# One program per engine for attention and FFN, and the short matmuls of a step in one group

## The reference

```python
q, k, v = (_causal_dwconv(_silu(xn @ W), conv_w) for W, conv_w in ...)   # 4 taps
z, a, b = xn @ Wz, xn @ Wa, xn @ Wb
q, k = rope and l2-normalise per head
for s in range(4):                                   # lags
    attn = sum_d(q * lag(k, s)) * scale
    out += (attn * sigmoid(lag(a, s) * b))[..., None] * lag(v, s)
rms = rsqrt(mean(out * out over all 2048 channels) + eps)
s = (out * rms * norm_w * _silu(z)) @ Wout
hidden = relu((xn @ sign(up_weight).T) * up_scale)
g = _silu((hidden @ sign(down_weight).T) * down_scale * output_scale)
return x + s * g
```

## Time and profile before

| | us |
|---|---|
| median of 3 runs (lowest, highest) | 1383.82 (1382.62, 1384.70) |
| the profiled execution, device time | 1383.09 |
| its span, first to last instruction | 1381.0 |
| start, until the steps run evenly (from the start) | about 74 |
| even steps, 14.10 each | 74 to 934 |
| seam between attention and FFN | 934 to 974 |
| FFN, then output | 974 to 1202, 1202 to 1371 |

### The profile page before, as it was taken

One profiled execution on the slowest core, in us unless ns is written; L12 is line 12 of the kernel. 1 busy time (PEld: TensorE's weight loads), 2 busy tenths in 40 slices (PEclk: granted clock), 3 DMA queues, 4 the chain that ended last, 5 costly groups with the idle time before them and its releaser, 6 DMA issues. The chain is left out here.

```text
span 1381.0 us, 23144 instructions
## 1 busy us (share of the span) xinstructions
PE 1350.4 (98%) x6824; PEld 1140.7 (83%) x6824; DVE 988.1 (72%) x1529; ACT 737.9 (53%) x2209; POOL 333.3 (24%) x508
## 2 busy tenths in 40 slices
PE   6999999999999999999999999996999999999998
PEld 4788888888888888888888888885888888888886
DVE  7898998989999999999998999983122222234443
ACT  5656665656656666666566665652654434432221
POOL 6134242323333232323333332422000000000001
PEclk9999999999999999999999999997999999999999
DMA  8233434334344344343433434333421101156454
GB/s 287 62 87 86 101 78 115 93 85 97 95 93 100 85 104 102 80 100 83 108 93 85 100 85 108 78 75 74 152 96 50 46 23 47 36 186 188 129 174 157
DMA packets 123418, 138.79 MB, mean 101 GB/s; under 512 B 30704, under 2 KB 67568, under 8 KB 123120
## 3 DMA queue, kind: packets, MB, share of 16 engines
q1 hardware_dynamic: 114160, 121.48, 31.1%
q0 software_dynamic: 9216, 16.78, 7.1%
HBM read 62.58 MB, written 25.30 MB: 64 GB/s over the span
## 5 line engine op out<-in xcount | busy, mean ns | idle before, releaser
L1169 DVE TENSOR_TENSOR hid_lo<-relu,hid_hi 128x512 fp32r<-128x512 f32 x64 | 44.3, 693 | 172.8 <-ACT hid_hi L1115 172.8
L670 DVE SCALAR_TENSOR_TENSOR y_v<-u_v,cw_v,y_v 128x512 f32<-128x512 f32 x192 | 144.8, 754 | 29.0 <-ACT y_v L561 24.3
L670 DVE SCALAR_TENSOR_TENSOR y_k<-u_k,cw_k,y_k 128x512 f32<-128x512 f32 x192 | 145.2, 756 | 26.1 <-ACT y_k L561 19.2
L581 ACT ACTIVATE bank<-bank 128x128 f32<-128x128 f32 x512 | 133.8, 261 | 46.7 <-PE bank L866 46.4
L670 DVE SCALAR_TENSOR_TENSOR y_q<-u_q,cw_q,y_q 128x512 f32<-128x512 f32 x192 | 144.1, 750 | 19.4 <-ACT y_q L561 10.5
L472 POOL TENSOR_TENSOR rq_win<-rq_win,const 128x32 f32<-128x32 f32 x64 | 21.4, 335 | 478.4 <-DMA rq_win<-rq_scratch 478.4
L1210 DVE TENSOR_TENSOR hid_lo<-o_raw,hid_hi 128x512 fp32r<-128x512 f32 x64 | 44.3, 692 | 101.4 <-ACT hid_hi L1135 101.4
L459 POOL TENSOR_TENSOR rnorm<-norms,neg_half 128x8 f32<-128x8 f32 x64 | 108.4, 1693 | 9.9 <-POOL norms L455 8.9
L1111 ACT ACTIVATE relu<-bank,us_sb 128x512 f32<-128x512 f32 x64 | 44.1, 689 | 121.9 <-PE bank L1250 121.9
L1135 ACT ACTIVATE hid_hi<-o_raw 128x512 fp32r<-128x512 f32 x64 | 40.4, 632 | 121.9 <-PE bank L1280 119.2
L1087 POOL TENSOR_TENSOR g_buf<-g_buf,up_raw 128x512 f32<-128x512 f32 x3 | 3.8, 1281 | 403.2 <-DVE g_buf L1190 403.2
(11 more groups left out here) (170 smaller groups left out, 3455.5 us busy)
## 6 DMA issues: line engine op xcount, KB each, us to landing
swapped_q<-y_q SPq DMA_DIRECT2D x128, 128.0 KB, 2.3
swapped_k<-y_k SPq DMA_DIRECT2D x128, 128.0 KB, 2.3
sq_sum<-out_sq POOLq DMA_DIRECT2D x64, 256.0 KB, 3.3
o_scratch<-o_buf SPq DMA_DIRECT2D x64, 256.0 KB, 2.6
o_raw<-o_scratch SPq DMA_DIRECT2D x64, 256.0 KB, 3.2
raw_q<-in_wq SPq DMA_DIRECT2D x16, 256.0 KB, 3.1
raw_k<-in_wk SPq DMA_DIRECT2D x16, 256.0 KB, 3.5
raw_v<-in_wv SPq DMA_DIRECT2D x16, 256.0 KB, 4.4
```

Source lines behind the costliest of these rows:

```text
L581: last = nc.scalar.activation(block_of, block_of, ACT.Square, accum_out=norms[:, g1 % 2, i * BC + b:i * BC + b + 1])
L670: nc.vector.scalar_tensor_tensor(y[n][:, g % 2, :], u[n][:, g % 2, i:i + CH], cw[n][:, bass.ds(h * TAPS + i, 1)], y[n][:, g % 2, :], ALU.m ...
L1169: nc.vector.tensor_tensor(hid_lo[:, j % 2, :], relu[:, j % 2, :], hid_hi[:, j % 2, :].bitcast(fp32), ALU.subtract).then_inc(hid_lo_done, 1)
```

## The change

- Attention and FFN become one program per engine, in one block. Semaphores are no longer freed between them; the tiles are laid out so that the FFN's first weights and hidden tiles lie where attention's projection weights lay.
- In a step, TensorE's order is now: transposes of q and k, projections q, k, v, z, transposes of v, values, scores.
- The square of the output waits for `o_buf`, and is made in the next step, ahead of v's silu; the values wait for it. The copy of the turned v and the saving of the spill go behind v's silu and z's silu on ScalarE.
- The tail is written out. TensorE: the last z projections, values of chunk 61, scores of 62, up 0, 1 and 2, scores of 63, values of 62, up 3, values of 63, then down 0, 1, 2, and from up 4 on the two alternate. The first chunk's ups and downs use other banks, and hidden tiles have four buffers instead of two.
- All sums of squares are made behind down 10 of the first chunk. The load of Wout's first group comes behind all FFN weights and all stores of o.
- In the start, the first q projection stands in three parts behind blocks 4, 5 and 6; a/b and k follow from block 7, and a third a/b projection fits between the transposes.

The diff, without changes of indentation, cut to its core:

```diff
-        ffn_and_output(nc, locals())
+        ffn = ffn_and_output(nc, locals())
+        att_sync, att_gpsimd, att_scalar, att_vector, att_tensor = attention(nc, locals())
+        ffn_sync, ffn_gpsimd, ffn_scalar, ffn_vector, ffn_tensor = ffn.programs
+        block = top.enter_context(nc.Block())
...
+        @block.tensor
+        def _(pe):
+            att_tensor(pe)
+            ffn_tensor(pe)
...
-            for g in range(3):
-                step(H, g)
...
+        store_rq(G - 1, NC)
+        load_rq(G - 2, NC)
+        load_rq(G - 1, NC, rq_last_in)
+        store_o(H - 1, G - 3, NC - 3)
+        ffn.load_weights(2)
+        ffn.load_weights(3)
+        store_o(H - 1, G - 2, NC - 2)
+        store_o(H - 1, G - 1, NC - 1)
...
+        roots(H - 1, G - 1, NC)
+        gate_keys(H - 1, G - 1, NC)
+        add_squares(0, NC - 4)
+        make_gates(G - 2, NC - 2)
+        make_gates(G - 1, NC - 1)
+        for g in (1, 2, 3):
+            add_squares(g, NC - 4 + g)
...
+        def square_out(k):
+            wait(act, o_done, k + 1)
+            wait(act, sq_added, 16 * k)
...
+        def step(h, g):
+            c = h * G + g
+            if at := back(h, g, 1):
+                square_qk(at[1], c)
+            if not is_start(h, g):
                 silu_and_tap("q", bank_qv, h, g, c)
                 silu_and_tap("k", bank_kz, h, g, c)
...
+            if back(h, g, 4):
+                square_out(c - 4)
             silu_and_tap("v", bank_qv, h, g, c)
...
+            elif g == 3:
+                for n in "qkvz":
+                    act.wait_ge(wlo_done[n], H)
+                ffn.up_signs(0)
+                ffn.up_signs(1)
+            if at := back(h, g, 2):
+                silu_z(at[1], c - 2, bank_kz)
+            if at := back(h, g, 1):
+                copy_v(at[1], c)
...
+            if at := back(h, g, 3):
+                save_spill(at[1], c)
...
+        square_qk(G - 1, NC)
+        square_out(NC - 4)
+        silu_z(G - 2, NC - 2, bank_kz)
+        copy_v(G - 1, NC)
+        save_spill(G - 3, NC)
+        silu_z(G - 1, NC - 1, bank_qv)
+        ffn.down_signs(0)
+        ffn.down_signs(1)
...
+        ffn.hidden(0, 0)
+        square_out(NC - 3)
+        ffn.hidden(0, 1)
+        save_spill(G - 2, NC + 1)
+        ffn.hidden(0, 2)
+        square_out(NC - 2)
+        ffn.hidden(0, 3)
+        save_spill(G - 1, NC + 2)
+        act.wait_ge(o_done, NC)
+        ffn.up_signs(2)
+        ffn.down_signs(2)
+        square_out(NC - 1)
...
+        join_out(G - 3, NC)
+        make_o(H - 1, G - 3, NC - 3)
+        ffn.split_hidden(0, 0)
+        gate_scores(G - 2, NC - 2)
+        mask_band(G - 2, NC - 2)
+        ffn.split_hidden(0, 1)
+        gate_scores(G - 1, NC - 1)
+        mask_band(G - 1, NC - 1)
+        join_out(G - 2, NC + 1)
+        make_o(H - 1, G - 2, NC - 2)
+        ffn.split_hidden(0, 2)
+        join_out(G - 1, NC + 2)
+        make_o(H - 1, G - 1, NC - 1)
+        ffn.split_hidden(0, 3)
...
+        early, late = range(TERMS // 2), range(TERMS // 2, TERMS)
         for b in range(NB):
             turn_x(b)
+            if BC <= b < BC + 3:
+                first_q(range((b - BC) * KT, (b - BC + 1) * KT))
+            elif b in (BC + 3, BC + 4):
+                project_ab(0, early if b == BC + 3 else late)
+            elif b in (BC + 5, BC + 6):
+                project("k", bank_kz, 0, 0, 0, early if b == BC + 5 else late)
...
             wait(pe, v_tok_done, c - 2)
             wait(pe, o_done, c - 3)
+            wait(pe, out_sq_done, c - 3)
...
-                if at1 and front:
-                    turn_v(at1[1], c)
-                if front:
                 wait(pe, silu_done["q"], 2 * c + 2)
                 project("v", bank_qv, h, g, c)
...
-                if at3 and front:
-                    sum_values(at3[1], c)
...
                 project("z", bank_kz, at2[0], at2[1], c - 2)
+            if at1:
+                turn_v(at1[1], c)
+            if at3:
+                sum_values(at3[1], c)
+            if at2:
+                score(at2[1], c - 2)
...
+        turn_qk(G - 1, NC)
+        wait(pe, z_done, NC - 2)
+        project("z", bank_kz, H - 1, G - 2, NC - 2)
+        turn_v(G - 1, NC)
+        wait(pe, silu_done["v"], 2 * NC)
+        project("z", bank_qv, H - 1, G - 1, NC - 1)
+        sum_values(G - 3, NC)
+        score(G - 2, NC - 2)
+        ffn.up(0, 0)
+        pe.wait_ge(z_done, NC - 1)
+        ffn.up(0, 1)
+        ffn.up(0, 2)
+        score(G - 1, NC - 1)
+        sum_values(G - 2, NC + 1)
+        ffn.up(0, 3)
+        sum_values(G - 1, NC + 2)
...
+    HS = 4
+    SQ_AT = 10
...
+        wait(dve, down_done, i - HS + 1)
...
+        for j in range(FT):
+            if j + 1 >= HS:
+                if j + 1 < FT:
+                    up(0, j + 1)
+                else:
+                    pe.wait_ge(out_sq_done, H * G)
+                    up(1, 0)
+            down(0, j)
+            if j == SQ_AT:
...
+                env["sum_squares"](bank_sq).then_inc(sq_total, 1)
```

More of the change, by code:

```diff
@@ L2 @@
 from concourse import mybir
+from collections import namedtuple
 from contextlib import ExitStack
@@ new lines, in attention @@
+    xt = [home.rearrange("p (b d) -> p b d", b=BC) for home in homes]
+    spare = flat(coef[:, :, :, :], 4)
+    stats = spare[:, 0:6 * NB].rearrange("p (b n) -> p b n", b=NB)
+    mean_var = spare[:, 6 * NB:8 * NB].rearrange("p (b n) -> p b n", b=NB)
+    rstd = spare[:, 8 * NB:9 * NB]
+    AHEAD = BC + 1
+    by_act = [b for b in range(NB) if b >= AHEAD and (b - AHEAD) % 2 == 0]
+    unused = y["v"]
+    ab_raw, ab_hi, ab_lo = raw["z"], w_hi["z"], w_lo["z"]
+    ab_t = rot["q"][0:AB, 0:S]
+    ab = out_sq[:, :].rearrange("p (b n) -> p b n", b=NB)
@@ new lines, in attention, with back @@
+    rq_masked = sem("rq_masked")
+    rq_joined = sem("rq_joined")
+    scores_done = sem("scores_done")
+    gates_done = sem("gates_done")
+    gated = sem("gated")
+    coef_done = sem("coef_done")
+    out_done = sem("out_done")
+    spill_saved = sem("spill_saved")
+    out_joined = sem("out_joined")
+    z_done = sem("z_done")
+    sq_asked = sem("sq_asked")
+    def back(h, g, k):
+        h2, g2 = (h, g - k) if g >= k else (h - 1, g - k + G)
+        if isinstance(h2, int) and not 0 <= h2 < H:
+            return None
+        return h2, g2
@@ L934, in ffn_and_output @@
+    return on_sync, on_gpsimd, on_scalar, on_vector, on_tensor
 def ffn_and_output(nc, env):
@@ new lines, in ffn_and_output, with is_first @@
+    o_in = [sem(f"o_in{i}") for i in range(WR)]
+    wo_hi_done = sem("wo_hi_done")
+    wo_lo_done = sem("wo_lo_done")
+    o_hi_done = sem("o_hi_done")
+    o_lo_done = sem("o_lo_done")
+    sq_total = sem("sq_total")
+    mean_done = sem("mean_done")
+    rms_done = sem("rms_done")
+    proj_used = sem("proj_used")
+    x_res_in = sem("x_res_in")
+    g_res_in = sem("g_res_in")
+    last_done = sem("last_done")
+    y_done = sem("y_done")
+    y_stored = sem("y_stored")
+    def is_first(n):
+        return isinstance(n, int) and n == 0
@@ new lines, in up_bank, with acc_of, out_chunks, load_weights @@
+    def up_bank(n, j):
+        return (up_first if is_first(n) else banks2)[j % 2]
+    def acc_of(n):
+        return acc_first if is_first(n) else acc
+    wout_at = {2 + 3 * t: t for t in range(KT)}
+    def out_chunks(eng, chunk):
+        second, first = acc_sets[1], acc_sets[0]
+        chunk(0, first, None)
+        with eng.Fori(0, G // 2 - 1) as m:
+            chunk(2 * m + 1, second, first)
+            chunk(2 * m + 2, first, second)
+        chunk(G - 1, second, first)
+    def load_weights(i):
+        wait(sp, up_signed, i - 1)
+        wait(sp, down_signed, i - 1)
+        load_ffn_weights(sp, i)
@@ new lines, in down @@
+    def down(n, j):
+        if is_first(n):
+            wait(pe, down_signed, j // WG + 1)
+        wait(pe, hid_lo_done, n * FT + j + 1)
+        for b in range(BC):
+            if j == 0:
+                wait(pe, acc_read, (n - 1) * BC + b + 1)
+            for part in (hid_hi, hid_lo):
+                last = nc.tensor.matmul(acc_of(n)[b], part[:, j % HS, b * P:(b + 1) * P],
+                                        down_group(j // WG)[:, j % WG, :], start=(j == 0 and part is hid_hi),
+                                        stop=(j == FT - 1 and part is hid_lo))
+        last.then_inc(down_done, 1)
```

2008 lines of the change are left out of this document (969 added, 1039 removed).

## The result

The changed kernel took 1370.87 us (median of 4 runs, 1369.19 to 1374.50) beside 1384.26 for the kernel before (4 runs): a ratio of 0.9908, 95% interval 0.9886 to 0.9930. The forecast was 1363.0 with a range to 1370: the direction was right, the gain of 13.4 us fell 7.4 short of the 20.8 foreseen, and the time came out 0.87 above the range. The profiled execution took 1370.76, with a span of 1368.8.

The account below looks back on a forecast made before the run. TensorE, busy 98% of the span, was taken as the bound. Span 1381.0 - 18.1 (seam) - 3.0 (steps) + 0.3 (start) = 1360.2; with 2.1 around it 1362.3, set against the median: 1363.0 us, range 1357 to 1370.

Parts of the forecast that it names:

- The bound: Whole kernel: TensorE is busy 98% of the span, so only its idle or slow time, or cheaper matmul order, can pay.
- The seam: From chunk 62's scores to the steady FFN: 20.1 of 31.78 us idle or slow; the new order takes 18.1 us less.
- a stall of 1.4 us remains: At the seam, TensorE waits 1.4 us ahead of values 63 for chunk 62's o and its square.
- it lands 3.3 later, at 9.5, 0.6 us ahead of its need: At the seam, the add of the previous square, issued at about 6.2, lands before chunk 62's square needs it.
- owes the sums of squares (3.6, and 0.1 for the switch): The sums of squares move from the seam to mid-FFN and cost 3.6 us plus 0.1 there.
- The rival on the clock: The clock falls in the seam's remaining stall, costing 3.5 us: 1366.5; chance 0.13.
- The step: Steady step: grouping short matmuls gains 0.05 us per step, 3.0 us less over 61 steps.
- The formula of the Trainium skill: Matmuls of one length get a fixed gap, N/2.4 plus 2.5 ns; by it a step's order would change nothing.
- "slower" rival: Each step, TensorE waits for ScalarE's copy of v; 0.35 us eats all gains, 0.85 gives 1393; chance 0.03.
- The start: First q projection in gaps of x's transposes wins 1.2; step 1's wait on v's copy loses 1.4, step 2 0.1; net 0.3 more.

Follow-up runs that it names:

- b_own_square: The changed kernel, with chunk 62's output square written to the free half of z's activation tile, so it needn't wait for the add before; 1366.98 us (one run).
- e_late_loads: a_align, with SyncE asking for weights of groups 2 and 3 only when the adds of squares of chunks 0 to 61 have landed; 1363.0 us (one run).
- a_align: The changed kernel with a pad shortened by 28 bytes, so sign tiles of weight groups 2 to 7 start at a multiple of 64 bytes; 1366.79 us, ratio 0.9886.
- h_shift64: The changed kernel with its pad sized so that both sign tiles of groups 2 to 7 start 64 bytes beyond a multiple of 128; 1370.83 us.
- i_before_all32: The kernel before, with all FFN tiles (up and down signs, hidden) 32 bytes beyond a multiple of 128, x at 0; 1393.97 us beside 1384.93.
- c_spread: The changed kernel with the sums of squares in four groups of eight behind down products 10 to 13, not one block; 1369.64 us, ratio 0.9911.
- f_old_order: a_align with TensorE's step in the old order: v's transposes between k and v projections, values ahead of z's; 1403.07 us, ratio 1.0138.
- j_best: The changed kernel with aligned sign tiles, chunk 62's square separate, a down product before the last values, sums in four groups, step 1's v transposes earlier; 1358.81 us.

## Why the prediction was right, and where it was not

The direction and the main mechanism held; the size did not, and the time came out past the range. What failed are three terms of the sum. The FFN's products were priced as before though their tiles had moved (4.7 us, no term for it); the add into the sums was given 3.3 us to land and took 6.0 (2.05 of stall); and the sums of squares were priced at the full clock only (3.1 in the profiled run).

- **The bound.** Right: the gain lay in idle and slow TensorE time at the seam; the three gaps went, and the FFN's first products fill them.
- **The seam, "a stall of 1.4 us remains".** The chain was right (1.35 in b_own_square and e_late_loads), the link behind it was not: "it lands 3.3 later, at 9.5, 0.6 us ahead of its need". It landed 6.0 us behind its issue, because the change itself puts 2 MB of weight loads on the DMA engines at that moment. The forecast named these loads and asked only whether they came in time for up 4, not what they do to the add. That is 2.05 us; the small waits of up 2, scores 63 and the first down product add 0.4, which makes the 19.66 against 17.2.
- **A term that is missing: where the tiles start.** The step that failed hardest. The sum prices up and down products at 1.81 ahead of up 4 and takes the FFN behind it as unchanged; it says nothing of the new places of the tiles, though the full diff has two new tiles behind a pad of odd size. From up 4 on the products took 1.86 to 1.87. It cost 4.7 us; a_align, h_shift64 and i_before_all32 show the cause. No row of the trace of before could have priced it, since the tiles of steps and FFN all start alike there.
- **"owes the sums of squares (3.6, and 0.1 for the switch)".** The price at the full clock is right (b_own_square: 3.5 and 0.1). But one block of them can lower the clock, and did: 3.1 us in the profiled run. The earlier trace rows showed two-column matmuls next to a falling clock, and the forecast blamed only the idle time. The rival on the clock had the mechanism and the wrong place. In its own place, behind the stall, the clock fell in four of nine profiles, for 1.6 us in c_spread instead of the 3.5 it names, but only behind stalls of 2.57 us and more; behind the 1.35 that it is about, the two profiles show no fall.
- **The step.** Right: 0.05 us each, 3.0 forecast, 2.85 measured between two orders in the same kernel, with 2.72 for the projections and 0.44 for v's transposes. The formula of the Trainium skill (TensorE: Matmul & The Clock Gate, section "Back-to-back issue gap"), which the section calls the gap of an isolated matmul, has no term for order. The runs don't follow it: the same twelve take 2.72 or 2.85 us by what precedes them. One price of the "slower" rival is wrong in its own arithmetic: 0.85 us in each of 61 steps is 52, which gives 1415 and not 1393. And a stall costs more than itself: with 0.35 a step f_old_order took 1403, 36 us over a_align, where the rival reckons 21.
- **The start.** Within its bounds: from the first transpose to step 2's q projection 54.0 us against 54.3, where 0.3 more was forecast and not 0.3 less; the copy of v costs 1.61 where 1.4 was forecast. The new places won 1.8 us (36.0 to 34.2 up to step 0's v projection) and not 1.2, and what follows up to step 2 lost 1.6, where 1.5 was forecast. The kernel's first transpose also came 0.7 earlier; it lies between 6.3 and 7.8 us in the profiles of this study, whatever the kernel.

In the profiled span: 4.7 for the tiles, 3.1 for the clock and 2.5 at the seam make 10.3 more than forecast; the start (0.7 and 0.6), the steps (0.2) and smaller items take 1.7 back: 8.6, the difference of 1368.8 and 1360.2.

## What to carry to other kernels

When a change moves transfers, ask not only whether they arrive in time but what lands beside them: a link with 0.6 us to spare, priced by a median, is no link to set to nothing. Thin matmuls belong between dense products in small groups, and a product that needs nothing new belongs in front of the work that waits for a long chain.

## What the chip showed that was not expected

- Matmuls of 128x512 in this format: 227 ns with weights and moving tile both at a multiple of 128 bytes, 229 to 230 with both off alike (32 or 64 bytes), 231 to 234 where they differ. Which of the two is off makes a difference of 1 to 2 ns at most. The cause is open.
- An add of 256 KB into SBUF landed in at most 3.35 us without the FFN's weight loads beside it, and in 6.0 and (at most) 8.95 beside 2 MB of them.
- The granted clock fell from its upper level (2.4 GHz) to the lower one with TensorE never idle, behind the 32 two-column matmuls in one block, in seven of nine profiles. Behind stalls of 2.57, 2.72, 3.28 and 3.69 us it fell too, behind others of 2.80, 2.94 and 3.45 it did not, nor behind the two of 1.35. The runs of kernels with such places spread over 2 to 5 us each, and those of j_best, which has none, over 0.8.
